# Moving the token factors and the down projection's low parts in the queues of a one-core feed-forward kernel

## What is computed

```
x = x + tanh(g_xattn) * cross_attention(layernorm(x), ctx, mask)      # x: 32 x 128 x 512, f32
h = silu(layernorm(x) @ w_gate) * (layernorm(x) @ w_up)               # 512 -> 2048
h = keep the 2 largest |h| of each 4 neighbours, zero the others
x = x + tanh(g_ffn) * (h @ w_down)                                    # 2048 -> 512
```

## Time and profile before

| | us |
|---|---|
| median of 3 runs | 1119.65 (1117.45 to 1120.14) |
| the profiled execution | 1116.94 |
| its span, first to last instruction | 1115.1 |
| TensorE matmul busy | 1082.4 (97%) |
| VectorE busy | 809.6 (73%) |
| ScalarE busy | 620.1 (56%) |
| DMA | 254.75 MB, mean 228 GB/s |
| mean granted clock of TensorE | 0.998 |

### The profile page before, as it was taken

How to read it: one execution, slowest core, us unless ns; L and a number is a source line. 1 busy time by engine, 2 the same in 40 slices (tenths; PEclk the granted TensorE clock), 3 DMA queues, 4 the chain that set the end, 5 groups by cost and what they waited for, 6 DMA issues and landing times.

```text
span 1115.1 us, 15146 instructions
## 1 busy us (share of the span) xinstructions
PE 1082.4 (97%) x4960; PEld 880.0 (79%) x4960; DVE 809.6 (73%) x1400; ACT 620.1 (56%) x1132; POOL 210.6 (19%) x328
## 2 busy tenths in 40 slices
PE   6998799999999999999999999999999999999998
PEld 5776587777878888888888888888888888888886
DVE  6999969879897757576775767675757565565765
ACT  5999678566765544454544444454445454443452
POOL 5576610121210111111111111001111111111111
PEclk9999999999999999999999999999999999999999
DMA  7899586798869977797779777888878666767726
GB/s 273 295 349 329 202 326 226 219 289 280 257 226 354 356 196 198 187 257 185 202 197 374 182 202 200 237 235 208 231 230 274 151 153 156 189 159 189 199 29 137
DMA packets 89533, 254.75 MB, mean 228 GB/s; under 512 B 9072, under 2 KB 9072, under 8 KB 85104
## 3 DMA queue, kind: packets, MB, share of 16 engines
q1 hardware_dynamic: 67856, 205.55, 52.2%
q0 software_dynamic: 21600, 48.24, 26.1%
HBM read 154.14 MB, written 99.61 MB: 228 GB/s over the span
## 4 chain that ended last, share of the span: by engine, by line
PE 73%; DVE 14%; ACT 4%; issue 4%; POOL 2%; DMA 2%; SPq 0%; DVEq 0%; ACTq 0%; POOLq 0%
PE ps_y L1302 9%; PE ps_a L1231 9%; PE ps_a L1233 9%; PE ps_a L1235 9%; PE ps_y L1304 9%; PE ps_y L1303 9%; PE ps_d L1233 4%; PE ps_d L1231 4%; PE ps_d L1235 4%; PE ps_c L1233 2%; PE ps_c L1231 2%; PE ps_c L1235 2%; DVE beats L980 2%; DMA w_raw<-in_L_ffn_w_up 1%; DVE x1n L930 1%
## 5 line engine op out<-in xcount | busy, mean ns | idle before, releaser
L569 POOL DMA_DIRECT2D out_rows<-y_out x124 | 107.1, 871 | 735.2 <-ACT y_out L717 712.7
L1231 PE MATMUL ps_a<-xm,w_ring 128*128 128x512 f32 x512 | 200.7, 392 | 3.6 <-ACT cp L597 3.3
L1233 PE MATMUL ps_a<-xm,w_ring 128*128 128x512 f32 x512 | 200.3, 391 | 0.0
L1235 PE MATMUL ps_a<-xm,w_ring 128*128 128x512 f32 x512 | 200.2, 391 | 0.0
L1302 PE MATMUL ps_y<-dn,h_hi 128*128 128x512 f32 x480 | 188.9, 394 | 4.4 <-ACT y_out L717 3.3
L1304 PE MATMUL ps_y<-dn,h_lo 128*128 128x512 f32 x480 | 187.4, 390 | 0.0
L1303 PE MATMUL ps_y<-dn,h_hi 128*128 128x512 f32 x480 | 187.0, 390 | 0.0
L717 ACT ACTIVATE y_out<-ps_y,ffn_gate 128x512 f32<-128x512 f32 x124 | 84.8, 686 | 158.4 <-PE ps_y L1304 158.3
L694 ACT ACTIVATE h_hi<-hidden 128x512 fp32r<-128x512 f32 x128 | 73.6, 626 | 107.0 <-DVE hidden L1006 107.0
L980 DVE TENSOR_TENSOR beats<-h_abs 128x512 bf16<-128x512 f32 x186 | 117.7, 684 | 1.3 <-ACT h_abs L687 1.3
L1231 PEld LDWEIGHTS ps_a<-xm,w_ring 128*128 128x128 f32 x512 | 96.4, 188 | 26.2 <-issue 5.2
(11 more groups left out here) (109 smaller groups left out, 1876.6 us busy)
## 6 DMA issues: line engine op xcount, KB each, us to landing
w_ring<-w_scratch SPq DMA_DIRECT2D x147, 512.0 KB, 4.5
out_rows<-y_out POOLq DMA_DIRECT2D x124, 256.0 KB, 4.3
w_scratch<-w_ring SPq DMA_DIRECT2D x56, 512.0 KB, 4.7
xm_scratch<-x_out SPq DMA_DIRECT2D x42, 512.0 KB, 5.4
xm<-xm_scratch SPq DMA_DIRECT2D x21, 1024.0 KB, 8.4
w_raw<-in_L_ffn_w_down SPq DMA_DIRECT2D x9, 1024.0 KB, 7.8
x_in<-in_x SPq DMA_DIRECT2D x32, 256.0 KB, 4.7
ctx_in<-in_ctx SPq DMA_DIRECT2D x32, 256.0 KB, 5.0
```

The lines of the kernel that those rows point to most:

```text
L569: nc.gpsimd.dma_start(out[RING * (n // (2 * TILES * QS)) + TILES * ORDER[order] + n % TILES], y_out[:, n % 4], accum_op=ALU.add).then_inc( ...
L1231: nc.tensor.matmul(to, w_ring[:, k, e, 0, c], xm[:, k, 0, c], start=begins and c == 0, stop=False, skip_group_check=not begins)
L1233: nc.tensor.matmul(to, w_ring[:, k, e, 0, c], xm[:, k, 1, c], start=False, stop=False, skip_group_check=not begins)
L1235: last = nc.tensor.matmul(to, w_ring[:, k, e, 1, c], xm[:, k, 0, c], start=False, stop=c == 1, skip_group_check=not begins)
```

## The change

It reorders instructions, and adds and removes none.

- ScalarE: x_high of point 3 goes from the end of the step into the next one, behind its two copy_a0. x_high of point 1 goes from the end of the even unit to behind the copy_a0 of the odd one. In odd units that build weights, spread(u + 1, 2) goes behind the two silu1.
- VectorE: x_low of point 3 goes into the next step, behind its add_c11 (in step 1 behind h_low). x_low of point 0 goes from in front of add_c22 to behind add_c22 and dn_low; dn_low goes in front of the last two comparisons. x_low of point 1 goes from the end of the even unit to behind add_c11 and w_low of the odd one.
- SyncE: where weights are built, the store of point 1 goes behind the last weight store of its unit.

```diff
@@ sync
                         for k in range(4):
                             store_w(u + 1, k)
-                        if half == 0:
-                            x_stored_at(s, 1)
                         for k in range(4, PROD):
                             store_w(u + 1, k)
-                        if half == 1:
-                            x_stored_at(s, 3)
+                        x_stored_at(s, 2 * half + 1)
@@ scalar, even unit
                     copy_a0(u, 1)
+                    x_high_at(s - 1, 3)
                     absolute(s - 1, 1, 2)
...
-                    x_high_at(s, 1)
@@ scalar, end of step 0, and of every later step
-                    x_high_at(0, 3)
...
-                x_high_at(s, 3)
@@ scalar, odd unit
                 copy_a0(u, 1)
+                x_high_at(s, 1)
...
                     w_high(act, u + 1, 0)
-                    spread(act, u + 1, 2)
                 silu1(u, 0)
                 silu1(u, 1)
                 if building:
+                    spread(act, u + 1, 2)
                     w_high(act, u + 1, 1)
@@ vector, even unit, s > 1
                     add_c11(u, 0)
                     add_c11(u, 1)
+                    x_low_at(s - 1, 3)
                     for j in tiles:
                         h_low(s - 1, 0, j)
                     compare(s - 1, 1, first + second + REST[:2])
-                    x_low_at(s, 0)
                     add_c22(u, 0)
                     add_c22(u, 1)
-                    compare(s - 1, 1, REST[2:])
                     if s - 1 in DN_BUILT:
                         dn_low(s - 1)
+                    x_low_at(s, 0)
+                    compare(s - 1, 1, REST[2:])
                     count_wins(s - 1, 1)
@@ vector, even unit, s == 1
                         h_low(0, 0, j)
+                    x_low_at(0, 3)
                     compare(0, 1, first + second)
...
-                    x_low_at(s, 1)
@@ vector, odd unit
                         w_low(dve, nc.vector, u, k)
+                x_low_at(s, 1)
                 for j in tiles[2:]:
...
-                x_low_at(s, 3)
```

More of the change, by code:

```diff
@@ L1130, in _ @@
                     keep(0, 0, kept_order(0))
-                    x_low_at(0, 3)
                     continue
```

## The result

The changed kernel took **1133.19 us** (median of four runs, 1131.55 to 1139.25) where the kernel before, on the same chip, took 1119.15 (four runs, 1117.45 to 1120.14): ratio 1.0127, 95% interval 1.009 to 1.0164, +14.0 us (the interval is 10 to 18 us). In two later sessions the same kernel took 1129.19 and 1129.45 (ratios 1.0096 and 1.0095, intervals 1.0067 to 1.0124 and 1.0078 to 1.0113). All 14 runs together have a median of 1130.6, about +12. The forecast was +6.6 us. All these executions were in the same, fast state.

The account below looks back on a forecast made before the run. TensorE bounds the kernel from step 4 on, with no slack on the y chain; VectorE and ScalarE's queue hold pair 0. Terms +0.8 + 4.2 + 1.6 = +6.6 us on 1119.65 gave 1126.2 us, range 1119 to 1133.

Parts of the forecast that it names:

- part 4: End of pair 0: x_blk lands about 0.3 us later, TensorE at step 4 +0.8 us late, bounds -1.5 and +2.5.
- Part 2: Steps 5, 6, 9, 10: down projection's load queued behind the moved x(s,3) lands 0.4 us late each; 1.6 us lost.
- part 1: Steps 6, 7, 8, 10, 11: x_low(s,0) behind add_c22 delays the y chain 0.6 or 1.2 us each; 4.2 us lost.
- part 3: Pair 0: nothing won by unit 3, then VectorE's waits for x_high go; TensorE 2.7 us ahead at unit 7.
- One wait of about 6 us: Unit 2: TensorE idles some 6 us from 188 us for copy_d0, behind x_high(1,0); VectorE absorbs it by unit 3.
- 2.8 us of weight stores through: Pair boundary: three weight stores that shared the engines at 345 to 348 us are through, 2.8 us set against later loads.
- (c): Rival: part 2's load keeps 7.8 us or more, four steps lose 1.7 us each; +11.8, 1131.5 us; chance 0.13.
- (a): Rival: pair 0's gain survives the boundary, x_blk lands 3 us earlier; +3.6 or about +1; chance 0.20 shared with (d).
- (b): Rival: faster, pair 0's waits are only ScalarE's queue, x_blk lands before 373 us; 1112 to 1116 us; chance 0.12.

Follow-up runs that it names:

- e9: The changed kernel itself, run again in a later session: 1129.45 us, ratio 1.0095 to the kernel before; its profiled execution took 1129.05 us.
- e6: Changed kernel with the down projection's load issued ahead of the store of point 3 in SyncE's queue: 1126.36 us, ratio 1.0075 to the kernel before.
- e7: Kernel before, with only dn_low ahead of the last two comparisons and x_low of point 0 behind it, from step 4 on: 1125.43 us, ratio 1.0058.
- e5: The changed kernel itself, run again as yardstick in a later session: 1129.19 us, +10.5 us over the kernel before.
- e16: Kernel before, with only x_high/x_low of point 3 moved to the next unit, from step 4 on: 1119.18 us, ratio 1.0008.
- e14: Kernel before, with the new order in steps 0 to 3 only and x(3,1) at its old place: 1117.71 us, ratio 0.999.
- e15: Kernel before, with the new order in steps 0 to 3 only and x(0,3) and x(3,1) at their old places: 1118.35 us, ratio 0.9998.
- e10: Changed kernel with matmuls into a free PSUM bank put into TensorE's waits, second run: 1129.87 us, ratio 1.0106 to the kernel before.
- e4_best: Kernel before, with only spread behind silu1 and some moves of dn_low and points 0, 1, 3 in steps 1 to 3: 1117.64 us, ratio 0.9997.
- the first half alone: Kernel before, with the new order in steps 0 to 3 only; with all its moves 1123.43 us, ratio 1.0045.
- e13: Kernel before, with the new order in steps 0 to 3 only and x(0,3) at its old place: 1121.94 us, ratio 1.0027.
- e11: Changed kernel with x(3,1) back at its old place at the end of unit 6: 1130.22 us.
- the sum of 16.7: Median losses of two kernels added: new order in steps 0 to 3 only (+5.7 us) and from step 4 on only (+11.0 us).

## Why the prediction was wrong in size

The direction and the places were right; the size was half of what came, and the measured time lies just above the upper end of the range. The step that failed is part 4, the pair boundary: +0.8 us was forecast there, and 4.4 came in the mildest profile. Part 2 was 1.0 us too small as well. Term by term, with e9 as the execution near the median:

| term | forecast, us | measured |
|---|---|---|
| part 1, x_low(s,0) on the y chain | 4.2 | waits of 4.06 in e6 and e7; TensorE 4.9 later for them in e7 |
| part 2, late load | 1.6 | 2.6 by e9's waits, 2.8 in the medians (e5 to e6); 0.7 without dn_low ahead (e16) |
| part 3, TensorE at unit 7 | 2.7 ahead | 0.6 ahead; 1.7 and 5.4 late in two other executions |
| part 4, behind unit 8 | +0.8 | +4.4; +6.3 and +11.0 in the others |
| sum | +6.6 | +12.1 in the trace; +10.5 to +14.0 in the medians |

**Part 1 held.** 0.57 and 1.17 us against 0.6 and 1.2, in exactly the five steps named, and the y chain without slack. TensorE falls behind by 0.13 to 0.2 us more than each wait: 0.77, 1.31, 0.77, 0.70 and 1.31 us in e7, 4.9 in sum. The prolonged matmul isn't the reason, for it takes 0.50 us before as well. Most of it is the way of counting: matmuls start 0.227 us apart but each row lasts 0.39 us, and the wait is counted from the end of the last row, 0.16 us later.

**Part 2: the right mechanism, a landing taken too short, and its cover not seen.** In e9 the load is issued 4.8 us later relative to TensorE (forecast 4.9). The landing was taken as 6.5 us; the four loads that count landed after 6.9, 6.8, 6.7 and 6.6 us, 1.0 us more in sum, and that is the difference of 2.6 and 1.6. The Trainium skill ("DMA: Bandwidth & Descriptors", Bandwidth) has 6.15 us for a copy of 1 MB; by it nothing would have been lost, and these four landings don't agree with it. One sentence failed too: "Swapping dn_low with two comparisons costs nothing in these steps". The forecast let dn_low start right behind add_c22 and so had the effect of the swap in its sum, but it put all of it down to the load. These comparisons were 1.28 us of cover: with them in front the same late load costs 0.7 us (e16), without them 2.6 to 2.8.

**Part 3 was right in what it absorbed, wrong in what it won.** One wait of about 6 us was forecast and 5.74 to 5.78 measured; that it is caught up is shown by e14 beside e15. It isn't caught up "by unit 3", but one unit later: in e14 +3.9 at unit 3, +0.7 at unit 4. The 2.7 us ahead at unit 7 became 0.6 and 0.7 in the better executions (e9, e14) and a lateness in the others, and by the scatter named above even 0.6 can't be told from nothing. The statement that VectorE is at 17 to 20 of 20 us in pair 0 was read from too few windows: it is busy 13.95 us from 220 to 240 and 15.49 from 280 to 300. I had walked through VectorE's queue alone; at the end of unit 3 TensorE waits for copy_y, which stands behind a `spread` that waits for a weight load, and that load's landing changes from execution to execution (TensorE waits 0.2 to 3.8 us there in the profiles without fill). The spread begins at 234.72 in the kernel before (TensorE waits 1.84 us), at 235.45 in e9 (0.35 us), and in the longest execution of the changed kernel (2.35 us, with slowed matmuls behind it) at 237.40:

```profile
237.40 1.11 ACT L290 ACTIVATE w_blk<-w_raw 128x512 f32<-128x512 f32 x1 [3.87 <-DMA w_raw<-in_L_ffn_w_up]
```

**Part 4 is the term that was mis-sized, by two steps.** Its geometry was right: x_low(3,1) was forecast at 342.2 with TensorE 2.7 ahead, so 344.9 with it on time. It stands at 344.35 with TensorE 0.6 ahead in e9 and at 350.35 with it 5.4 late in the longest execution, 344.95 both. The first step that failed is the lead of part 3 (2.1 us in e9). The second is the term "2.8 us of weight stores through". From the first token load to x_high(4,0) it is 31.0 us before and 31.2 in e9, 30.9 in the longest execution, so none of the 2.8 us came in these. Over all 18 profiles of this study it is 30.3 to 33.1 us (mean 31.9) in the nine with the old order of the stores and 29.3 to 31.4 (mean 30.6) in the nine with the new one: about 1.3 us of the term came on average, less than the executions differ by. SyncE and ScalarE of e9:

```profile
345.07 1.11 SPq L387 DMA_DIRECT2D xm_scratch<-x_out  x1
350.81 5.05 SPq L418 DMA_DIRECT2D xm<-xm_scratch  x7
...
382.04 0.63 ACT L342 ACTIVATE x_out<-x_blk 128x512 fp32r<-128x512 f32 x1 [6.79 <-DMA x_blk<-xnT_scratch]
```

First load +3.4, landing +3.55 us, not +0.3. Behind it there is only 0.7 us of room: product 5 of unit 8 starts 1.26 us after x_high(4,0) begins whenever it waits (383.30 in e9, 380.43 in e14), and 2.00 after it before. TensorE is 2.8 us late there, and slowed matmuls behind the wait bring it to 4.5 at the down projection; the forecast left them out for the new waits though it counted those of the old one. The y chain hangs on the same landing, which I had named but not costed as a start: add_c22 adds to what copy_d0 writes. VectorE of e9:

```profile
383.25 1.29 DVE L950 TENSOR_TENSOR hidden<-ps_a,hidden 128x512 f32<-128x512 f32 x2 [5.82 <-ACT hidden L667]
```

Before it ran from 379.76, so the whole chain starts 3.49 us late, and copy_y of tile 0 comes 3.9 us late (x_low(4,0), 0.6 us, stands between). In e9 TensorE is later than that already and doesn't wait for it. In e10, without slowed matmuls, it does, 0.77 us; and in e7, which has nothing new ahead of unit 8 but a landing 1.9 us late by chance, step 4 costs 1.5 us. The two ways meet at tile 2, and the later counts.

**The rivals.** (c) was right that the sum is nearer to 12 than to 7, but not in its reason: no load kept 7.8 us or more in all four steps and lost 6.8. (a) holds for e9's lead only; it doesn't survive the boundary. (b) didn't come: even e14 and e4_best, which keep moves of pair 0 and avoid the costs, are within 0.1% of the kernel before. x_high(4,0) began at 378.95 us at the earliest (e15), not before 373. The rule of the Trainium skill that stood beside it ("Perfetto Trace Analysis", Optimization Strategy: find what blocks the busiest engine and make it start sooner) brought nothing here.

**Open.** Why keeping x(3,1) gains 3.6 us in the first half alone (e13 to e15) and nothing in the median of the whole changed kernel (e9 to e11). e11's x_blk lands at 379.7 and its wait in unit 8 is gone, but that execution was 3.4 us late at unit 7 already and waits 1.00 us at tile 2 of step 4 instead. The means of the six runs each differ by 0.1 us, give or take 2.8, so a gain of 2 us could be hidden there, all of 3.6 hardly. That x_low(4,0) and a late x_blk meet in one unit, where the later counts, would fit both this and the sum of 16.7; it is argued, not shown.

## What to carry to other kernels

A step moved on a queue needs two checks: who waits for it now, and what it used to cover; a late load that is nearly free by itself can cost once a second edit takes away what covered it. Where the next stage begins with a chain of transfers that starts when the last factor is stored, look first at the place of that one store: here it cost 3.6 us, while a stall of 5.7 us inside the stage cost nothing. An instruction put on a chain without slack costs its own length: here 0.70 to 0.77 us for one of 0.60 and 1.31 for two, which can be forecast to 0.2 us. And one profile is one execution: before a lead of 1 or 2 us enters a sum, see how far two executions of the same order differ.

## What the runs showed of the hardware

- The chain from the issue of the first of seven token loads (1 MB each) to the start of x_high(4,0), which waits for the load of 1 MB behind them, took 29.3 to 33.1 us in the 18 profiles. In nine of them the last three weight stores were issued 0.9 to 2.5 us ahead of it and landed after it had begun: mean 31.9 us. In the other nine they were issued 5.5 to 8.9 us ahead and had landed: mean 30.6 us.
- A wait of 5.7 to 5.8 us was followed by matmuls at the lower clock, six to thirteen of them 0.43 us apart, in each of seven profiles, and the same wait filled with 24 matmuls by none. Shorter waits were followed by such a stretch in some executions and not in others, and their length alone doesn't decide: 1.86 us in step 7 of e5_after_again was, 1.87 in the same step of e9 wasn't, nor were 2.98 us in unit 3 of e7 and 3.02 in e4_best.
- Matmuls start 0.227 us apart while each row lasts 0.39 us, so a wait read between rows is 0.16 us shorter than the gap in the stream of matmuls.
- Executions of one kernel on one chip differ by some 5 us: 1127.12 to 1132.26 for six of the changed kernel, 1116.61 to 1122.39 for seventeen of the kernel before. In the three profiled executions of the changed kernel 6.0 of the 10.2 us between the longest and the shortest stand at unit 7 already.
